# Context attention on one core: score maxima issued eight tiles ahead over each block border, and the second shift turn taken into the preceding block

## The chip, the cores and the metric

The kernel is one program on one core of a Trainium2 chip. The metric is the device time of one execution in microseconds (us). TensorE (PE) does the matmuls and loads their weights (PEld), VectorE (DVE) the reductions, ScalarE (ACT) exponentials and copies. GpSimd and the DMA queues play no part in the stage that is changed.

## The reference, cut to what matters

The program is a two-layer decoder on 1024 tokens of 128 features. The changed stage is the first layer's context attention: 16 heads of 8 features look at 6404 context rows, and all heads share one key and one value projection.

```python
c = jnp.concatenate([mem, kv], axis=1)           # both are the same context
qh = (q @ w_q).reshape(B, L, N_HEAD, D_HEAD).transpose(0, 2, 1, 3)
kvp = c @ w_kv
k, v = (kvp[..., :D_HEAD], kvp[..., D_HEAD:])
attn_score = jnp.einsum('bhid,bjd->bhij', qh, k) / np.sqrt(D_HEAD)
attn_prob = jax.nn.softmax(attn_score, axis=-1)
out = jnp.einsum('bhij,bjd->bhid', attn_prob, v)
```

The two halves of the concatenation are equal, so softmax over one of them gives the same output. The kernel computes exp(score - row maximum) and divides by the sum at the end, so every row's maximum must be known before its exponentials start.

## The kernel before

All of the change lies in `context_attention` (L712). The work is cut into 16 blocks (`NB`), each 8 heads of 128 tokens, so 1024 query columns. Even blocks have their queries and keys on partitions 0 to 63, odd blocks on 64 to 127 (`rows`, L810).

A block needs two passes over the context. The **maximum pass** has 104 tiles (`TILES`), 8 heads by 13 ranges of up to 512 context rows, the last range of a head being 260 wide. `max_tile` (L830) is one matmul on 64 partitions into one of four PSUM places (`PLACES`), and `maximum` (L1065) on VectorE reduces it. After tile 51 and after tile 103, `negate` (L1072) turns the maxima of four heads into a negative shift, in halves A and B. `turn_shift` (L838) transposes such a half with four PE instructions into a place of its own, and `take_shift` (L856) copies it on ScalarE into two rows of the query stack, so that the later score matmul subtracts the maximum by itself.

The **score pass** has 102 steps (`EXPS`): 51 chunks of 128 context rows by 2 halves of the query columns. `score` (L967) is one matmul on 64 partitions into one of three PSUM banks, the exponential of it follows on ScalarE (`exponentiate`, L1045), and `weigh` (L956) multiplies a chunk's probabilities with the values, four column strips at a time. Waits of this pass: score e waits for exponential e - 3 (its bank); scores 0 and 1 of a block wait for shifts A and B; a chunk's first exponential waits for `weigh` of three chunks earlier (the probabilities have three buffers); `weigh` of a chunk waits for both its exponentials. The program order on PE is written out in `attend` (L1015): after step e come the items that `items_at` holds for it, then two `weigh` after each step e with e mod 6 = 2, and one after each with e mod 6 = 5. After step 101 the `weigh` of the last but one chunk follows too, and the very last one comes after step 0 of the next block. After exponential 0 ScalarE takes the finished sums of the block before (`take_acc`, L1041).

Both passes run side by side: while block b is scored, the maxima of block b + 1 are computed. These blocks have different parity, so their matmuls use different halves of the partitions. The 103 tiles 1 to 103 are spread over steps 0 to 99; turn A stands after step 57; tile 0 of block b + 2 comes after step 101, and turn B of block b + 1 after the last `weigh` of block b. Its copy by ScalarE follows exponential 101. The maxima of block 0 come before all scores, from `q_first`, mixed with matmuls and copies for layer 1 (`first_job`, `copy_job`); four of these jobs are held back for the time around turn B of block 0. A place is given in the order of issue (`order`, `place`): the item issued four later waits until it was used (`free_place`, L818), a tile by its reduction, a turned shift by its copy. VectorE takes tiles and negations in strict order. Block 15 has no tiles beside it; there each token tile is finished instead (`finish_tile`).

Of the kernel before, what the change touches and what calls it, by code (L numbers as in the profile page):

```python
# [31 lines left out]
NCH = -(-CTX // P)  # L32
# [679 lines left out]
def context_attention(k):  # L712
# [18 lines left out]
    with ctx:  # L731
# [3 lines left out]
        with ExitStack() as tmp:  # L735
# [11 lines left out]
            shift_ready = {"A": k.sem("shift_a_ready"), "B": k.sem("shift_b_ready")}  # L747
# [25 lines left out]
            NJOBS = KEYS + len(val_jobs)  # L773
            EARLY_JOBS = NJOBS
            HELD = 4
            late_jobs = list(range(EARLY_JOBS, NJOBS))

            TURN_AT, LAST_AT, FIRST_TURN = 28, NCH - 1, 66  # L780
            first = [(0, u) for u in range(FIRST_TURN + 1)] + [(0, "A")] + [(0, u) for u in range(FIRST_TURN + 1, TILES)]


            def border(b):
                return [(b + 1, 0)] if b + 1 < NB else [], [(b, "B")]

            items_at = []
            job_at = {}
            for b in range(NB):
                todo = list(range(1, TILES)) if b + 1 < NB else []  # L790
                count = len(todo)
                for c in range(NCH):
                    now = ([], [])
                    if todo and c < LAST_AT:
                        for j in range(2):
                            n = (count * (2 * c + j + 1)) // (2 * LAST_AT) - (count * (2 * c + j)) // (2 * LAST_AT)
                            now[j].extend((b + 1, u) for u in todo[:n])
                            del todo[:n]
                        if c == TURN_AT:
                            now[1].append((b + 1, "A"))  # L800
                    if late_jobs and c in (12, 38):
                        job_at[b * NCH + c] = late_jobs[0]
                        now[1].append(("job", late_jobs.pop(0)))
                    if c == NCH - 1 and b + 1 < NB:
                        now[1].extend(border(b + 1)[0] + border(b + 1)[1])
                    items_at.append(now)
            order = first + border(0)[0] + border(0)[1] + [x for now in items_at for half in now for x in half]
            place = {x: i for i, x in enumerate(order)}

            def rows(blk):  # L810
# [4 lines left out]
            def bank(item):  # L815
                return max_ps[:, place[item] % PLACES, :]

            def free_place(pe, item):  # L818

                if place[item] < PLACES:  # L820
                    return
                blk, what = order[place[item] - PLACES]
                if blk == "job":
                    pe.wait_ge(job_copied, what + 1)
                elif what in shift_ready:
                    pe.wait_ge(shift_ready[what], blk + 1)
                else:
                    pe.wait_ge(tile_used, blk * TILES + what + 1)
# [17 lines left out]

            def issue(pe, item):
                free_place(pe, item)
                if item[0] == "job":
                    layer1_job(pe, item[1], bank(item))  # L850
                elif item[1] in shift_ready:
                    turn_shift(pe, *item)
                else:
                    max_tile(pe, *item)
# [55 lines left out]
            def layer1_job(pe, i, to):  # L910

                if i < KEYS:
                    c0, cols = key_jobs[i]
                    ins = nc.tensor.matmul(to[:, 0:cols], k.wk1[:], k.ctx_T[:, c0:c0 + cols], start=True, stop=True)
                else:
                    c, m = val_jobs[i - KEYS]
                    n = P if c < NCH - 1 else TAIL
                    for j in range(m):
                        ins = nc.tensor.matmul(to[0:n, j * D:(j + 1) * D], k.ctx_T[:, (c + j) * P:(c + j) * P + n],
                                               k.wv1[:], start=True, stop=True)  # L920
                ins.then_inc(job_ready, 1)
# [93 lines left out]
            def attend(pe, blk):  # L1015

                for e in range(EXPS):
                    score(pe, blk, e)
                    items = items_at[blk * NCH + e // JOBS][e % JOBS]
                    for item in items:  # L1020
                        if item[1] != "B":
                            issue(pe, item)
                    of = e // 6 * 3
                    if e == 0 and blk > 0:
                        weigh(pe, blk - 1, NCH - 1)
                    elif e % 6 == 2 and of > 0:
                        weigh(pe, blk, of - 2)
                        weigh(pe, blk, of - 1)
                    elif e % 6 == 5:
                        weigh(pe, blk, of)  # L1030
                    if blk == NB - 1 and e in TURNED_AT:
                        turn_heads(pe, TURNED_AT[e])
                    if blk == NB - 1 and e in BACK_AT:
                        turn_back(pe, BACK_AT[e])
                    if blk == NB - 1 and e in PROJECTED_AT:
                        project(pe, PROJECTED_AT[e])
                weigh(pe, blk, NCH - 2)
                if blk + 1 < NB:
                    issue(pe, (blk + 1, "B"))

            def take_acc(act, blk):  # L1041
                act.wait_ge(pv_done, (blk + 1) * NCH)
# [2 lines left out]
            def exponentiate(act, blk):  # L1045
                for c in range(NCH):
                    n = P if c < NCH - 1 else TAIL
                    if not (blk == 0 and c < 3):
                        act.wait_ge(pv_done, blk * NCH + c - 2)
                    for j in range(JOBS):  # L1050
                        e = c * JOBS + j
                        act.wait_ge(score_ready, blk * EXPS + e + 1)
                        nc.scalar.activation(probs[0:n, c % 3, j * HALF:(j + 1) * HALF], score_ps[0:n, e % 3, :],  # L1053
                                             ACT.Exp).then_inc(exp_done, 1)
                        if e == 0 and blk > 0:
                            take_acc(act, blk - 1)
                    if c == TURN_AT and blk + 1 < NB:
                        take_shift(act, nc.scalar.copy, blk + 1, "A")
                    if blk * NCH + c in job_at:
                        i = job_at[blk * NCH + c]  # L1060
                        copy_job(act, i, bank(("job", i)))
                if blk + 1 < NB:
                    take_shift(act, nc.scalar.copy, blk + 1, "B")

            def maximum(dve, blk, u):  # L1065

# [18 lines left out]
            with nc.Block() as block:  # L1085
                @block.tensor
                def _(pe):
# [19 lines left out]
                            issue(pe, (0, "A"))  # L1107
                    for i in held_jobs[0:2]:
                        first_job(pe, i)
                    for item in border(0)[0] + border(0)[1]:  # L1110
                        issue(pe, item)
                    for i in held_jobs[2:4]:
                        first_job(pe, i)
# [1288 lines left out]
```

## Time and profile before

| what | value |
|---|---|
| median of three runs | 2043.5 us (2041.26 to 2043.7) |
| span of the profiled execution, first to last instruction | 2039.6 us |
| its busy shares: PE, VectorE, ScalarE | 96%, 77%, 66% |
| mean granted TensorE clock | 0.986 |
| first exponential of block 0, of block 15 | 256.8 us, 1215.4 us |
| copies of shift B, block 0 to block 15 | 255.1 us to 1214.8 us: 15 blocks of 63.98 us |

The profiled execution's own device time is not listed; the timed runs are 1.7 to 4.1 us above its span, which is what lies around the first and the last instruction. A busy share is an average over stages, and PE's ends are modelled because its matmuls are pipelined: starts say more than ends. In a timeline row the figures are the start, the length (of the whole merged stretch, with its count), and in brackets how long the engine had been idle and what ended that. "Idle <-X" names who was waited for. Block and step numbers are not in the rows; they follow from counting the instructions of a line.

### The profile page before, as it was taken

What the parts mean: (1) busy time and instruction counts of PE and PEld (TensorE: products, weight loads), DVE (VectorE), ACT (ScalarE), POOL (GpSimd) and SP (SyncE); (2) the same over time, 40 slices, a digit from 0 to 9 for tenths busy, and PEclk for the clock granted to TensorE, in tenths of its full rate; (3) what the DMA queues carried; (4) which work ended last, traced back from release to release, by engine and by line L of the source; (5) the groups of instructions that cost most, each with busy time, mean ns of one, the idle gap of its engine ahead of it and who ended that gap; (6) DMA issues with size and microseconds to landing.
All of it is one profiled execution on the core that took longest, in us unless ns stands there. A gap on an engine that the chain in (4) does not pass through costs nothing. (4 is left out here: it accounts for less than half of the span.)

```text
span 2039.6 us, 36001 instructions
## 1 busy us (share of the span) xinstructions
PE 1959.2 (96%) x14245; PEld 969.3 (48%) x14245; DVE 1573.2 (77%) x2868; ACT 1355.8 (66%) x2394; POOL 100.9 (5%) x85
## 2 busy tenths in 40 slices
PE   7779999999999999999999999999999998999997
PEld 2225744444444444444444444444344444777755
DVE  7997899999999999999999981233688865444344
ACT  5333488888888888888888887432578874443321
POOL 1661000000000000000000000000200000000000
PEclk8999999999999999999999999999999999999999
DMA  4210000000000000000000000232000000000000
GB/s 148 73 62 0 1 2 2 2 1 2 1 1 2 2 1 2 2 2 1 1 2 1 2 2 1 60 120 65 0 1 1 2 1 0 1 1 1 16 29 28
DMA packets 25043, 32.66 MB, mean 16 GB/s; under 512 B 5967, under 2 KB 20335, under 8 KB 24622
## 3 DMA queue, kind: packets, MB, share of 16 engines
q1 hardware_dynamic: 23694, 28.30, 4.5%
q8 instruction: 111, 1.82, 0.4%
q10 hardware_dynamic: 1184, 2.10, 0.3%
q14 instruction: 54, 0.44, 0.1%
HBM read 29.61 MB, written 0.65 MB: 15 GB/s over the span
## 5 line engine op out<-in xcount | busy, mean ns | idle before, releaser
L1069 DVE TENSOR_REDUCE sb_max_partial<-ps_max_ps 128x1 f32<-128x512 f32 (+1 forms) x1664 | 977.3, 662 | 43.9 <-PE ps_max_ps L836 43.1
L1053 ACT ACTIVATE sb_probs<-ps_score_ps 128x512 f32<-128x512 f32 (+1 forms) x1632 | 875.1, 597 | 117.6 <-PE ps_score_ps L974 71.7
L974 PE MATMUL ps_score_ps<-sb_q_stack,sb_key_stack 64*128 64x512 f32 x1632 | 586.6, 443 | 3.9 <-ACT sb_probs L1053 3.4
L836 PE MATMUL ps_max_ps<-sb_key_stack,sb_q_stack 64*128 64x512 f32 (+1 forms) x1560 | 555.9, 438 | 0.0
L963 PE MATMUL ps_acc_ps<-sb_probs,sb_val_ones 128*32 128x256 f32 x6528 | 465.0, 387 | 0.0
L974 PEld LDWEIGHTS ps_score_ps<-sb_q_stack,sb_key_stack 64*128 64x128 f32 x1632 | 275.8, 183 | 321.5 <-ACT sb_probs L1053 257.2
L836 PEld LDWEIGHTS ps_max_ps<-sb_key_stack,sb_q_stack 64*128 64x128 f32 x1560 | 265.0, 184 | 9.8 <-DVE sb_max_partial L1069 7.5
L963 PEld LDWEIGHTS ps_acc_ps<-sb_probs,sb_val_ones 128*32 128x32 f32 x6528 | 156.3, 108 | 207.7 <-issue 140.5
L1721 DVE TENSOR_REDUCE sb_s_max_partial<-ps_s_ps 128x1 f32<-128x512 f32 x256 | 158.5, 682 | 24.6 <-PE ps_s_ps L1567 24.5
L1708 ACT ACTIVATE sb_s_probs<-ps_s_ps 128x512 f32<-128x512 f32 x256 | 140.8, 597 | 30.8 <-PE ps_s_ps L1595 22.8
L1942 DVE TENSOR_SCALAR_CACHE_REDUCE sb_x_scores<-ps_x_score_ps 128x1024 f32<-128x1024 f32 (+1 forms) x56 | 62.0, 1110 | 69.2 <-PE ps_x_score_ps L1929 69.2
L1977 ACT COPY sb_x_turned<-ps_x_turn_ps 128x512 f32<-128x512 f32 (+1 forms) x52 | 29.5, 568 | 116.8 <-PE ps_x_turn_ps L1967 116.8
L1987 PE MATMUL ps_x_acc_ps<-sb_x_turned,sb_val 128*128 128x256 f32 (+1 forms) x408 | 105.4, 381 | 0.0
L1567 PE MATMUL ps_s_ps<-sb_s_key_stack,sb_s_q_stack 64*128 64x512 f32 x256 | 103.5, 462 | 1.9 <-DVE sb_s_q_stack L1521 1.5
L1595 PE MATMUL ps_s_ps<-sb_s_q_stack,sb_s_key_stack 64*128 64x512 f32 x256 | 103.4, 464 | 0.3 <-ACT sb_s_q_stack L1699 0.2
L1929 PE MATMUL ps_x_score_ps<-sb_key_T,sb_x_q_T 128*128 128x512 f32 (+1 forms) x208 | 97.7, 579 | 1.8 <-DVE sb_x_scores L1942 1.8
L1300 DVE TENSOR_TENSOR sb_e_hidden<-sb_e_hidden,sb_e_gate_rows 128x1024 f32<-128x1024 f32 x30 | 36.7, 1226 | 75.6 <-ACT sb_e_hidden L1292 60.3
L471 PE MATMUL ps_mamba_ps<-sb_xpad,sb_ident 128*128 128x512 f32 x128 | 65.2, 632 | 23.0 <-POOL sb_xpad L536 23.0
L640 ACT ACTIVATE sb_val<-sb_delta,sb_a_neg 128x1024 f32<-128x1024 f32 x32 | 36.6, 1148 | 74.0 <-DVE sb_key_T L697 69.3
L1292 ACT ACTIVATE sb_e_hidden<-ps_e_hid_ps,sb_e_b 128x1024 f32<-128x1024 f32 x34 | 37.9, 1113 | 71.4 <-PE ps_e_hid_ps L1268 71.4
L1606 PE MATMUL ps_s_ps<-sb_s_probs,sb_s_val_ones 128*32 128x256 f32 x1024 | 81.8, 391 | 0.2 <-ACT sb_s_probs L1708 0.2
L536 POOL TENSOR_TENSOR sb_xpad<-sb_key_T,sb_val 128x1024 f32<-128x1024 f32 x31 | 73.9, 2383 | 58.3 <-DVE sb_key_T L697 57.2
(299 smaller groups left out, 1802.7 us busy)
## 6 DMA issues: line engine op xcount, KB each, us to landing
sb_val<-c_rows SPq DMA_DIRECT2D x16, 512.0 KB, 3.6
sb_e_gate_rows<-e_gate_dram SPq DMA_DIRECT2D x15, 512.0 KB, 3.9
sb_e_w<-L_ffn_rW SPq DMA_DIRECT2D x30, 128.0 KB, 2.1
sb_e_w<-L_ffn_W_T SPq DMA_DIRECT2D x24, 128.0 KB, 2.1
sb_ctx_T<-ctx_T SPq DMA_DIRECT2D x1, 1664.0 KB, 7.6
sb_ctx_T<-ctx_T ACTq DMA_DIRECT2D x1, 1538.0 KB, 8.6
sb_x_T<-x_T SPq DMA_DIRECT2D x1, 512.0 KB, 3.8
sb_x_tok<-x ACTq DMA_DIRECT2D x1, 512.0 KB, 11.0
```

What stands on the lines that cost most here:

```text
L836: nc.tensor.matmul(bank((blk, u))[:, 0:n], queries, keys, start=True, stop=True).then_inc(tile_ready, 1)
L963: ins = nc.tensor.matmul(acc_ps[32 * q:32 * q + 32, 0:QUART], k.val_ones[:, v, :], probs[:, v % 3, q * QUART:(q + 1) * QUART], start=(v == ...
L974: nc.tensor.matmul(score_ps[:, e % 3, :], k.key_stack[rows(blk), c * P:(c + 1) * P], q_stack[rows(blk), blk // 2, j * HALF:(j + 1) * HALF] ...
L1053: nc.scalar.activation(probs[0:n, c % 3, j * HALF:(j + 1) * HALF], score_ps[0:n, e % 3, :], ACT.Exp).then_inc(exp_done, 1)
L1069: nc.vector.tensor_reduce(partial[:, blk % 2, h, r:r + 1], bank((blk, u))[:, 0:RANGES[r][1]], AX.X, ALU.max).then_inc(tile_used, 1)
L1567: nc.tensor.matmul(bank((blk, u)), q_stack[rows(blk), blk // 2, t * P:(t + 1) * P], key_stack[rows(blk), blk // 2, r * HALF:(r + 1) * HALF ...
L1595: nc.tensor.matmul(score_ps[:, n % 3, :], key_stack[rows(blk), blk // 2, c * P:(c + 1) * P], q_stack[rows(blk), blk // 2, j * HALF:(j + 1) ...
L1606: ins = nc.tensor.matmul(acc_ps[32 * q:32 * q + 32, 0:QUART], val[:, v, head(blk), :], probs[:, n % BUFS, q * QUART:(q + 1) * QUART], star ...
L1708: nc.scalar.activation(probs[:, n // 2 % BUFS, (e % 2) * HALF:(e % 2 + 1) * HALF], score_ps[:, n % 3, :], ACT.Exp).then_inc(exp_done, 1)
L1721: nc.vector.tensor_reduce(partial[:, blk % 2, t, r:r + 1], bank((blk, u)), AX.X, ALU.max).then_inc(tile_used, 1)
L1929: ins = nc.tensor.matmul(score_ps[:, at % 2, (i % 2) * HALF:(i % 2) * HALF + n], q_T[:, t * P:(t + 1) * P], k.key1_T[:, i * HALF:i * HALF ...
L1987: ins = nc.tensor.matmul(acc_ps[:, p % 2, 0:2 * P], k.val1[0:keys, c, :], turned[0:keys, G % DEPTH, 2 * j * P:2 * (j + 1) * P], start=(c = ...
```

## The change

- The tiles of the next block but one that are issued within a block grow from 1 to 8 (`LEAD` + `KEEP`): tiles 0 to 3, then turn B of the next block, then tiles 4 to 7.
- Turn B is one item of the list now, no longer issued after the block's last `weigh`. Its copy on ScalarE follows the second exponential of the chunk in which the turn stands (`shift_at`), no longer exponential 101.
- Turn A stands after tile 57 (`TURN_AFTER`). Items of a block are spread evenly, 106 over 102 steps. That puts turn A alone after step 49, tiles 58 and 59 both after step 50, tile 103 after step 93, tiles 0 to 3 of block b + 2 after steps 94 to 97, turn B after step 98, tiles 4 and 5 after steps 99 and 100, 6 and 7 both after step 101.
- Block 14, which has no block but one after it, spreads 98 items over 96 steps (`LAST_SLOTS`): tile 103 and turn B both stand after step 95.
- Before block 0 the list around turn B grows in the same way: tiles 0 to 3 of block 1, turn B of block 0, tiles 4 to 7, between held jobs 2 and 3.
- Code for late jobs goes; there were none (`EARLY_JOBS = NJOBS`).

```diff
-            TURN_AT, LAST_AT, FIRST_TURN = 28, NCH - 1, 66
+            TURN_AFTER, FIRST_TURN = 57, 66
+            LEAD, KEEP, LAST_SLOTS = 4, 4, 96
             def border(b):
-                return [(b + 1, 0)] if b + 1 < NB else [], [(b, "B")]
+                ahead = [(b + 1, u) for u in range(LEAD + KEEP)] if b + 1 < NB else []
+                return ahead[:LEAD] + [(b, "B")] + ahead[LEAD:]
...
+            items_at, shift_at = [], {}
             for b in range(NB):
-                todo = list(range(1, TILES)) if b + 1 < NB else []
...
+                todo = []
+                if b + 1 < NB:
+                    todo = [(b + 1, u) for u in range(LEAD + KEEP, TURN_AFTER + 1)] + [(b + 1, "A")]
+                    todo += [(b + 1, u) for u in range(TURN_AFTER + 1, TILES)] + border(b + 1)
+                slots = EXPS if b + 2 < NB else LAST_SLOTS
+                for e in range(EXPS):
+                    now = todo[len(todo) * e // slots:len(todo) * (e + 1) // slots]
+                    shift_at.update({(b, e // JOBS): what for _, what in now if what in shift_ready})
                     items_at.append(now)
...
                 for e in range(EXPS):
                     score(pe, blk, e)
-                    items = items_at[blk * NCH + e // JOBS][e % JOBS]
-                    for item in items:
-                        if item[1] != "B":
-                            issue(pe, item)
+                    for item in items_at[blk * EXPS + e]:
+                        issue(pe, item)
...
                 weigh(pe, blk, NCH - 2)
-                if blk + 1 < NB:
-                    issue(pe, (blk + 1, "B"))
...
-                    if c == TURN_AT and blk + 1 < NB:
-                        take_shift(act, nc.scalar.copy, blk + 1, "A")
...
-                if blk + 1 < NB:
-                    take_shift(act, nc.scalar.copy, blk + 1, "B")
+                    if (blk, c) in shift_at:
+                        take_shift(act, nc.scalar.copy, blk + 1, shift_at[blk, c])
...
-                    for item in border(0)[0] + border(0)[1]:
+                    for item in border(0):
                         issue(pe, item)
```

## Rows read from the trace of the kernel before

**Rows 1.** Busy time by stretch: length, PE, PEld, DVE, ACT, POOL, clock, DMA; block 8.

```profile
768.01:831.94 63.93, 63.51 (x630) 29.05 (x622) 61.90 (x111) 55.97 (x106) 0.00 (x0) 1.00 0.01 2
```

**Rows 2.** Groups by line and shape, block 2: count, busy, mean ns, idle before.

```profile
L1069 DVE TENSOR_REDUCE sb_max_partial<-ps_max_ps 128x1 f32<-128x512 f32 x97 | 59.4, 683 | 2.4 <-PE ps_max_ps L836 2.4
```

**Rows 3.** Who waited for whom, whole span: us in total, times, longest.

```profile
PEld ps_score_ps L974 <- ACT sb_probs L1053: 257.2, 683, 0.6
...
PEld ps_max_ps L836 <- DVE sb_max_partial L1069: 12.0, 62, 0.4
```

**Rows 4.** Timeline of VectorE (start, length, count, idle before): border into block 3.

```profile
448.27 0.69 DVE L1069 TENSOR_REDUCE sb_max_partial<-ps_max_ps 128x1 f32<-128x512 f32 x1 [0.64 <-PE ps_max_ps L836]
449.28 15.18 DVE L1069 TENSOR_REDUCE sb_max_partial<-ps_max_ps 128x1 f32<-128x512 f32 x26 [0.31 <-PE ps_max_ps L836]
```

**Rows 5.** Timeline of PE and ACT, block 3, from after step 26 to after step 32.

```profile
463.05 1.07 PE L963 MATMUL ps_acc_ps<-sb_probs,sb_val_ones 128*32 128x256 f32 x16
464.05 0.49 PE L974 MATMUL ps_score_ps<-sb_q_stack,sb_key_stack 64*128 64x512 f32 x1
464.06 0.50 PE L836 MATMUL ps_max_ps<-sb_key_stack,sb_q_stack 64*128 64x512 f32 x1
464.39 0.39 PE L974 MATMUL ps_score_ps<-sb_q_stack,sb_key_stack 64*128 64x512 f32 x1
464.62 0.39 PE L974 MATMUL ps_score_ps<-sb_q_stack,sb_key_stack 64*128 64x512 f32 x1
464.95 0.64 PE L963 MATMUL ps_acc_ps<-sb_probs,sb_val_ones 128*32 128x256 f32 x8
465.52 0.50 PE L974 MATMUL ps_score_ps<-sb_q_stack,sb_key_stack 64*128 64x512 f32 x1
466.21 0.18 PEld L974 LDWEIGHTS ps_score_ps<-sb_q_stack,sb_key_stack 64*128 64x128 f32 x1 [0.30 <-ACT sb_probs L1053]
466.65 1.07 PE L963 MATMUL ps_acc_ps<-sb_probs,sb_val_ones 128*32 128x256 f32 x16
467.35 0.60 ACT L1053 ACTIVATE sb_probs<-ps_score_ps 128x512 f32<-128x512 f32 x1 [0.15 <-PE ps_acc_ps L963]
```

**Rows 6.** Timeline at the border from block 3 to block 4, from step 98 on.

```profile
507.69 1.07 PE L963 MATMUL ps_acc_ps<-sb_probs,sb_val_ones 128*32 128x256 f32 x16
...
509.04 0.28 PE L836 MATMUL ps_max_ps<-sb_key_stack,sb_q_stack 64*128 64x260 f32 x1
...
509.26 0.39 PE L974 MATMUL ps_score_ps<-sb_q_stack,sb_key_stack 64*128 64x512 f32 x1
509.26 0.18 PEld L836 LDWEIGHTS ps_max_ps<-sb_key_stack,sb_q_stack 64*128 64x128 f32 x1
509.49 0.39 PE L836 MATMUL ps_max_ps<-sb_key_stack,sb_q_stack 64*128 64x512 f32 x1
...
511.08 0.60 PE L843 MATMUL ps_max_ps<-sb_ident,sb_neg_part 128*2 128x128 f32 x4 [0.20 <-DVE sb_neg_part L1082]
...
511.71 0.57 ACT L861 CAST sb_q_stack<-ps_max_ps 2x512 fp32r<-2x512 f32 x1 [0.95 <-PE ps_max_ps L843]
...
512.31 0.60 ACT L1053 ACTIVATE sb_probs<-ps_score_ps 128x512 f32<-128x512 f32 x1
...
513.13 0.60 ACT L1053 ACTIVATE sb_probs<-ps_score_ps 128x512 f32<-128x512 f32 x1
```

**Rows 7.** Timeline of PE around turn A, after step 57 of block 1.

```profile
355.04 0.60 PE L843 MATMUL ps_max_ps<-sb_ident,sb_neg_part 128*2 128x128 f32 x4
355.56 0.49 PE L974 MATMUL ps_score_ps<-sb_q_stack,sb_key_stack 64*128 64x512 f32 x1
```

**Rows 8.** Timeline around turn B of block 0, ahead of the first score.

```profile
254.47 0.60 PE L843 MATMUL ps_max_ps<-sb_ident,sb_neg_part 128*2 128x128 f32 x4
254.58 0.69 DVE L1069 TENSOR_REDUCE sb_max_partial<-ps_max_ps 128x1 f32<-128x512 f32 x1 [0.86 <-PE ps_max_ps L836]
254.91 0.61 PE L919 MATMUL ps_acc_ps<-sb_wv,sb_ctx_T 128*128 128x128 f32 x4
```

More of the change, by code:

```diff
@@ L775, in context_attention @@
             HELD = 4
-            late_jobs = list(range(EARLY_JOBS, NJOBS))
-            TURN_AT, LAST_AT, FIRST_TURN = 28, NCH - 1, 66
+            TURN_AFTER, FIRST_TURN = 57, 66
+            LEAD, KEEP, LAST_SLOTS = 4, 4, 96
             first = [(0, u) for u in range(FIRST_TURN + 1)] + [(0, "A")] + [(0, u) for u in range(FIRST_TURN + 1, TILES)]
             def border(b):
-                return [(b + 1, 0)] if b + 1 < NB else [], [(b, "B")]
-            items_at = []
-            job_at = {}
+                ahead = [(b + 1, u) for u in range(LEAD + KEEP)] if b + 1 < NB else []
+                return ahead[:LEAD] + [(b, "B")] + ahead[LEAD:]
@@ L789, in context_attention @@
+            items_at, shift_at = [], {}
             for b in range(NB):
-                todo = list(range(1, TILES)) if b + 1 < NB else []
[L791 to L805, printed above, removed]
+                todo = []
[6 more added lines that the diff above has]
+                    shift_at.update({(b, e // JOBS): what for _, what in now if what in shift_ready})
@@ L806, in context_attention @@
                     items_at.append(now)
-            order = first + border(0)[0] + border(0)[1] + [x for now in items_at for half in now for x in half]
+            order = first + border(0) + [x for now in items_at for x in now]
             place = {x: i for i, x in enumerate(order)}
@@ L822, in free_place @@
                 blk, what = order[place[item] - PLACES]
-                if blk == "job":
-                    pe.wait_ge(job_copied, what + 1)
-                elif what in shift_ready:
+                if what in shift_ready:
                     pe.wait_ge(shift_ready[what], blk + 1)
@@ L848, in issue @@
                 free_place(pe, item)
-                if item[0] == "job":
-                    layer1_job(pe, item[1], bank(item))
-                elif item[1] in shift_ready:
+                if item[1] in shift_ready:
                     turn_shift(pe, *item)
@@ L1056, in exponentiate @@
                             take_acc(act, blk - 1)
-                    if c == TURN_AT and blk + 1 < NB:
-                        take_shift(act, nc.scalar.copy, blk + 1, "A")
-                    if blk * NCH + c in job_at:
-                        i = job_at[blk * NCH + c]
-                        copy_job(act, i, bank(("job", i)))
-                if blk + 1 < NB:
-                    take_shift(act, nc.scalar.copy, blk + 1, "B")
+                    if (blk, c) in shift_at:
+                        take_shift(act, nc.scalar.copy, blk + 1, shift_at[blk, c])
             def maximum(dve, blk, u):
```

## The prediction, made before the changed kernel ran

> **What bounds the kernel now.** I read the stretches first. A block lasts 63.9 us, and within one VectorE is busy 61.9 us, ScalarE 56.0 us, PE 63.5 us [rows 1]. So VectorE looks like the bound, with 2.4 us of idle in front of full tiles in a block [rows 2], most of it at the border: 0.64 and 0.31 us, after which 26 tiles run without a gap at 0.58 us each [rows 4]. That idle is what the change can take away. Then I asked who holds PE back. If VectorE set the pace, tiles would wait for their places. They did 62 times in the span, 12.0 us in all, about four times and 0.8 us in a block; score loads waited for exponentials 683 times, 257.2 us [rows 3]. So I followed one period of six steps [rows 5]. From the double weigh at 463.05 to the next at 466.65 it is 3.60 us, and it closes on itself without VectorE: the score at 466.21 waits for an exponential, the weigh follows 0.44 us later, and the exponential at 467.35 waits for that weigh. Seventeen such periods are 61.2 us. The loop between PE and ScalarE is thus the bound, and VectorE's 61.5 us (63.9 less 2.4) lies just under it. VectorE's gaps at the border are in large part the loop's own delay, seen from the side.
>
> Relative to a double weigh at 0, a period on PE reads [rows 5]: score and tile at 1.00, 1.34 and 1.57 (a pair after a pause takes 0.34, later ones 0.23), single weigh at 1.90, scores at 2.47 and 2.81, the third at 3.16 because it waits, double weigh at 3.60, its exponential 0.70 later. A tile costs PE nothing here: it starts 0.01 us after the score beside it, since the two use different partitions.
>
> **The change part by part.**
>
> Tiles 0 to 7 of block b + 2 have block b's parity, so they stand on the partitions of the scores they are issued between. Before, one tile a block did: it started 0.23 us after its score, not 0.01 [rows 6]. Now eight do. The two after step 101 and the ones after 99 and 100 meet other waits (below); those after steps 94 to 97 lie in one period. With score and tile 103 at 1.00: score 1.34, tile 1.57, score 1.80, tile 2.03, weigh 2.36, score 2.93, tile 3.27 (0.34 after the pause), score 3.50, tile 3.73, score 98 at 3.96 in place of 3.16. PE's slack in the period was about 0.1 us, so 0.80 arrives. Bounds: 0 if pipelining hid it all, 8 x 0.23 = 1.84 if nothing were hidden anywhere; I take 0.80, the row-by-row sum.
>
> The Trainium skill ("TensorE: Matmul & The Clock Gate", Part 3, The mechanism) says that a weight load overlaps running matmuls only when its row group differs. By that, each such tile would also pay its load, 0.18 us. Here the trace disagrees: the tile's load started with the score at 509.26 on the same partitions, and the tile 0.23 us later [rows 6]. By the rule the border would cost 4 x 0.18 = 0.7 us more; I leave it out of the sum.
>
> Turn B, four PE instructions, moves in front of the double weigh after step 98. Turn A shows its price: 0.52 us from its start to the next pair [rows 7]. Before the weigh it takes the place of a pair that took 0.44: score 3.96, turn 4.29, weigh 4.82. Against 3.60 that is +1.22, and exponential 98 is as late. The turn's place was tile 0's, so it also waits until VectorE has reduced that tile. Tile 103 is in PE at 1.00, VectorE needs its start-up, the negation and tile 0: before, turn B came 2.04 us after tile 103 with the negation between [rows 6], so tile 0 ends at about 1.00 + 2.04 + 0.6 = 3.6, ahead of 4.29. The bound is 0 to 0.6 (one tile late); I take 0.
>
> From the double weigh to the next block: before, 507.69 to exponential 0 at 512.31, 4.62 us, with 0.95 us of ScalarE idle for turn B, and exponential 1 at 5.44 [rows 6]. After: score 99 at 1.00, tile 1.34, score 1.57, tile 1.80, score 2.03, tile 2.27; exponential 99 at 1.53; ScalarE copies B from 2.02 to 2.60 (0.57, rows 6). Tile 7 has B's place, so PE waits for this copy, and behind it in PE's queue stand two weighs and score 0: tile at 2.65, weighs from 3.09 (0.44), score 0 at 4.09, its exponential at about 4.6. The same as before: ScalarE idles about as long, for another reason. Then the last weigh at 4.53, score 1 at 5.10, exponential 1 at 5.62, that is +0.18. VectorE meanwhile runs dry between tiles 3 and 4 and waits again for tile 8, so it brings no lead into the next block: the 1.0 us at the border [rows 4] isn't gained but moved.
>
> Inside a block the work is the same. Turn A keeps its price but stands ahead of a step that carries two tiles and a double weigh, up to 0.5 worse; the steps with two items fall from four to three, and up to 0.8 us of place waits [rows 3] could go. I take -0.1, with -0.8 and +0.5 as ends.
>
> So a border costs 1.22 + 0.18 - 0.1 = 1.3 us, at 14 borders (out of blocks 0 to 13) 18.2 us.
>
> Before block 0, turn B of block 0 now waits for tile 0's reduction, at 254.58 + 0.69 = 255.27 in place of 254.47 [rows 8]. Tile 6 waits for tile 3's reduction, three tiles of 0.6 later, 257.1; tile 7 follows at 257.35, and the two held jobs, which had started at 254.91, at about 257.6. Their copies and the first score wait for them: +2.7 us. Ends 0.8 (only the turn) and 3.
>
> In block 14 turn B follows tile 103 in the same step 95, so PE and everything behind it wait through reduction and negation: turn at 1.57 + 2.04 = 3.61, single weigh at 4.14 in place of 1.90. The double weigh comes at about 5.6, +2.0; the border after it, without turn and tiles, takes about 3.5 to exponential 0 in place of 4.62. Together +1.0, ends -1 and +2.
>
> The sum is 18.2 + 2.7 + 1.0 = 21.9 us. The span of 2039.6 goes to 2061.5; the median stands 3.9 above the span, and nothing outside the stage changes, so 2043.5 + 21.9 = 2065 us. With the ends of the terms, the border between 0.6 and 1.8, it is 8.4 + 0.8 - 1 = 8 to 25 + 3 + 2 = 30, that is 2052 to 2074. Dropped copies and turns: none; the removed late jobs issued nothing, and no DMA moves.
>
> **The rivals.**
>
> VectorE is the bound after all. It stands at 61.9 of 63.9 us [rows 1], and its tiles run at 0.58 us, which makes six in a period of 3.60 hardly distinguishable from the loop's own [rows 4, 5]. Then eight tiles ahead cover the border, and a block loses the 0.95 us of gaps and the cold restart, about 1.1. It decides wherever a score waits behind a tile that waits for its place. Fifteen borders give -17, less 1 to 3 at the start: 2028 us. Against it stand the four place waits in a block. The Trainium skill ("Perfetto Trace Analysis", Identifying the Most-Contended Engine) takes the engine with the highest occupancy as the one to relieve, judging PE by its weight loads; that rule gives this rival.
>
> The unpaired tiles hide in PE's pauses, and the border is neither better nor worse: only turn B's 0.4 and the start remain, gained back by fewer place waits. For it: PE's pauses are long elsewhere. Against: the period has none where the tiles fall. Sum near 0 to +4: 2045 us.
>
> The change doesn't loosen anything and tightens more: turn B waits for a late VectorE (0.6 a border) and the extra items of steps 25, 50 and 76 delay the loop by 0.24 each [rows 6]. That adds 1.3 a border to my 1.3: 2083 us.
>
> The weight loads of tiles on the scores' partitions are exposed: 0.18 us each [rows 6], four in the critical period, 14 borders, 10 us more than my sum: 2075 us. The row above speaks against it, since that load ran beside the score. The rule of the Trainium skill's page "TensorE: Matmul & The Clock Gate" gives this case.
>
> **How the numbers follow.** My forecast has 0.62, VectorE as the bound 0.18, no effect 0.12, the worse case 0.06, exposed loads 0.02. What can be told from no change is 0.2%, 4 us. Faster gets 0.19 (the first rival and a little of the third), same 0.10, slower 0.71. The range for 8 in 10 reaches down through the case of no effect and up to the edge of the worse case: 2039 to 2079; the likeliest case alone has 2052 to 2074.
>
> **What would show it.** Right: blocks of 65.2 us between shift copies in place of 63.98; score and tile starts 0.23 apart at eight tiles of a block; the double weigh after step 98 about 4.8 us after the one before; ScalarE still idle about a microsecond ahead of exponential 0, now behind a weigh and a score; VectorE dry over a microsecond between tiles 3 and 4; the first exponential 2.7 us later. Wrong: blocks under 63.5 us with VectorE running through the border, or a double weigh after step 98 on time, which would mean that the tiles on the same partitions cost PE nothing.

## The result and the profile after

The changed kernel takes 2103.7 us (median of four executions, 2074.4 to 2116.7), the kernel before on the same chip 2043.6 (2041.3 to 2045.2). It is slower by 60 us, where 21.9 had been forecast. The ratio on record is 1.020, with a 95% interval of 1.015 to 1.026. Ratios here and below leave out executions that were set apart as slow, which keeps 2074.4 and 2094.6 here and 2062.6 and 2078.4 in e7, so that the medians of these two sets give more, 1.029 and 1.022. The executions of the changed kernel differ by up to 42 us, for a reason that the profile shows below, so the time at which one is read has to be named: the profiled one took 2112.8 us, its span is 2111.1 (before: 2039.6), its mean granted TensorE clock 0.958 (before: 0.986).

First the clock row of both pages: the span in 40 slices, the granted clock in tenths of full speed. Before, then after:

```profile
PEclk8999999999999999999999999999999999999999
```

```profile
PEclk8999999999999999999999965799999999999999
```

Before, the whole stage shows 9. After, three slices show 6, 5 and 7. These lie at 1214 to 1372 us, where blocks 14 and 15 end the stage. Stretches of the changed kernel: length, busy time of PE, PEld, VectorE, ScalarE and GpSimd, granted clock, DMA. They are block 8, block 14 and block 15 (first exponential to first exponential, block 15 to its last), and the end of block 14 by itself (counts of instructions in brackets):

```profile
782.95:848.12 65.17, 64.82 (x626) 30.47 (x622) 61.90 (x111) 56.22 (x105) 0.00 (x0) 1.00 0.01 1
1174.16:1242.85 68.69, 66.34 (x617) 29.17 (x613) 57.18 (x102) 56.04 (x105) 0.00 (x0) 0.94 0.00 1
1242.85:1356.61 113.76, 113.76 (x558) 47.82 (x554) 10.41 (x42) 56.67 (x103) 0.00 (x0) 0.54 0.00 1
1233.90:1242.85 8.95, 8.95 (x54) 3.49 (x55) 0.00 (x0) 3.81 (x7) 0.00 (x0) 0.51 0.00 0
```

And block 15 of the kernel before:

```profile
1215.37:1284.20 68.83, 68.61 (x558) 31.81 (x550) 10.44 (x42) 55.54 (x103) 0.00 (x0) 1.00 0.01 1
```

Block 15 has the same 558 matmuls and 103 ScalarE instructions before and after. It takes 68.8 us at a granted clock of 1.00 (2.4 GHz) and 113.8 at 0.54, so nearly all of it at 1.2 GHz, with PE shown as busy all the time. By blocks the 71.5 us of span went here:

| stretch | before | after | difference | forecast |
|---|---|---|---|---|
| tile 0 of block 1 on PE to the first exponential | 2.79 | 6.65 | +3.9 | +2.7 |
| blocks 0 to 13, together | 894.65 | 913.45 | +18.8 | +18.2 |
| block 14 | 63.89 | 68.70 | +4.8 | +1.0 |
| block 15 | 68.83 | 113.76 | +44.9 | 0 |
| all else | | | -0.9 | 0 |

The border was as forecast. Timeline of PE, ScalarE (ACT) and VectorE (DVE) of the changed kernel from the double weigh after step 92 of block 3 to the first exponential of block 4 (start, length of the stretch, idle before):

```profile
512.56 1.07 PE L951 MATMUL ps_acc_ps<-sb_probs,sb_val_ones 128*32 128x256 f32 x16
...
513.90 0.39 PE L962 MATMUL ps_score_ps<-sb_q_stack,sb_key_stack 64*128 64x512 f32 x1
514.13 0.39 PE L826 MATMUL ps_max_ps<-sb_key_stack,sb_q_stack 64*128 64x512 f32 x1
514.36 0.39 PE L962 MATMUL ps_score_ps<-sb_q_stack,sb_key_stack 64*128 64x512 f32 x1
514.59 0.39 PE L826 MATMUL ps_max_ps<-sb_key_stack,sb_q_stack 64*128 64x512 f32 x1
...
516.84 0.60 PE L833 MATMUL ps_max_ps<-sb_ident,sb_neg_part 128*2 128x128 f32 x4
517.36 1.07 PE L951 MATMUL ps_acc_ps<-sb_probs,sb_val_ones 128*32 128x256 f32 x16
518.07 0.60 ACT L1037 ACTIVATE sb_probs<-ps_score_ps 128x512 f32<-128x512 f32 x1 [0.91 <-PE ps_acc_ps L951]
519.12 2.48 DVE L1048 TENSOR_REDUCE sb_max_partial<-ps_max_ps 128x1 f32<-128x512 f32 x4 [1.45 <-PE ps_max_ps L826]
519.51 0.57 ACT L849 CAST sb_q_stack<-ps_max_ps 2x512 fp32r<-2x512 f32 x1
520.57 1.07 PE L951 MATMUL ps_acc_ps<-sb_probs,sb_val_ones 128*32 128x256 f32 x16
522.15 0.69 DVE L1048 TENSOR_REDUCE sb_max_partial<-ps_max_ps 128x1 f32<-128x512 f32 x1 [0.54 <-PE ps_max_ps L826]
522.17 0.60 ACT L1037 ACTIVATE sb_probs<-ps_score_ps 128x512 f32<-128x512 f32 x1 [1.00 <-PE ps_score_ps L962]
```

Read it from the weighs. From 512.56 to 517.36 are 4.80 us, where a period takes 3.60 [rows 5]. In between, score and tile alternate 0.23 us apart, since both use the same partitions, and turn B (L833) stands in front of the second weigh. VectorE, which before ran 26 tiles without a gap from behind the border on [rows 4], is dry for 1.45 us there and for 0.54 us at the next tile. ScalarE idles 1.00 us before exponential 0, as it idled 0.95 before the copy of B [rows 6].

Then the place where the clock goes. PE in the changed kernel at the end of block 14, from tile 103 on:

```profile
1231.14 0.28 PE L826 MATMUL ps_max_ps<-sb_key_stack,sb_q_stack 64*128 64x260 f32 x1
1233.54 0.60 PE L833 MATMUL ps_max_ps<-sb_ident,sb_neg_part 128*2 128x128 f32 x4 [2.03 <-DVE sb_neg_part L1061]
1234.08 1.08 PE L951 MATMUL ps_acc_ps<-sb_probs,sb_val_ones 128*32 128x256 f32 x8
1235.09 1.64 PE L962 MATMUL ps_score_ps<-sb_q_stack,sb_key_stack 64*128 64x512 f32 x3
1236.66 1.93 PE L951 MATMUL ps_acc_ps<-sb_probs,sb_val_ones 128*32 128x256 f32 x16
```

Turn B of block 15 stands directly behind tile 103, so PE waits 2.03 us for VectorE's last tile and its negation. The next rows are already slow: a single weigh takes 1.08 us where it took 0.64, and a double one 1.93 where it took 1.07 [rows 5]. The trace has the clock at 1.2 GHz from 1234.0 on, for 112.6 us, that is until 1346.6, ten microseconds before the end of block 15.

### The profile page after: what moved, and what is told of

It is laid out like the page before. It is cut to its first block and busy times, and to the rows that moved or that the text cites. A ratio compares the mean times of both kernels' runs of the same rounds, so it can differ in the third digit from the quotient of the medians.

```text
span 2111.1 us, 36001 instructions
## 1 busy us (share of the span) xinstructions
PE 2030.3 (96%) x14245; PEld 1007.6 (48%) x14245; DVE 1573.1 (75%) x2868; ACT 1359.3 (64%) x2394; POOL 100.8 (5%) x85
## 5 line engine op out<-in xcount | busy, mean ns | idle before, releaser
L962 PE MATMUL ps_score_ps<-sb_q_stack,sb_key_stack 64*128 64x512 f32 x1632 | 613.8, 457 | 3.4 <-ACT sb_probs L1037 3.0
L951 PE MATMUL ps_acc_ps<-sb_probs,sb_val_ones 128*32 128x256 f32 x6528 | 486.3, 402 | 0.0
L962 PEld LDWEIGHTS ps_score_ps<-sb_q_stack,sb_key_stack 64*128 64x128 f32 x1632 | 287.9, 191 | 330.8 <-ACT sb_probs L1037 270.8
L471 PE MATMUL ps_mamba_ps<-sb_xpad,sb_ident 128*128 128x512 f32 x128 | 65.2, 632 | 22.8 <-POOL sb_xpad L536 22.8
```

Of the source, the lines that this page charges most:

```text
L951: ins = nc.tensor.matmul(acc_ps[32 * q:32 * q + 32, 0:QUART], k.val_ones[:, v, :], probs[:, v % 3, q * QUART:(q + 1) * QUART], start=(v == ...
L962: nc.tensor.matmul(score_ps[:, e % 3, :], k.key_stack[rows(blk), c * P:(c + 1) * P], q_stack[rows(blk), blk // 2, j * HALF:(j + 1) * HALF] ...
```

## The experiments

All times are medians, beside the kernel before on the same chip (2042.0 to 2043.9 us). Unless it says otherwise, an edit is one to the changed kernel. "Thin" stands for steps with a score but no tile beside it, so that the scores run on one half of the partitions with nothing on the other, as in all of block 15. A row of blocks has the columns of the stretches above.

### Is it the clock, and what makes it fall?

**e7, the changed kernel once more**, no edit, in a second set of runs.

> The changed kernel as it is, a second time, beside the next three. If the fall of the clock at the end of block 14 belongs to the program, most executions show block 15 near 110 us and times from 2075 to 2115 again (theory P+Q: the wait of 2.0 us together with six steps without tiles). If it was the chip's mood that day (R), the time is about 2066 and block 15 takes 69 us.

2087.1 us (2062.6 to 2123.3), ratio 1.014 (1.009 to 1.019). Blocks 14 and 15 of the profiled execution, which took 2123.3 us:

```profile
1175.51:1244.61 69.10, 66.75 (x617) 29.26 (x613) 57.20 (x102) 56.04 (x105) 0.00 (x0) 0.93 0.00 1
1244.61:1364.74 120.13, 120.13 (x550) 50.16 (x550) 10.42 (x42) 56.88 (x103) 0.00 (x0) 0.50 0.00 1
```

The fall comes again, 1.2 GHz for 133 us this time, and block 15 is 6 us longer still. The kernel before, beside it on the same chip, took 2040.8 to 2045.8 us in seven executions, so it isn't the chip alone. The wait is the same to the hundredth:

```profile
1234.89 1.01 PE L833 MATMUL ps_max_ps<-sb_ident,sb_neg_part 128*2 128x128 f32 x4 [2.03 <-DVE sb_neg_part L1061]
```

The trace has the clock down from 1234.69 on, 0.20 us before this turn starts. So the clock fell within PE's wait, before anything behind it had run. In the first profile it fell 0.46 us behind the wait's end, when PE had begun nothing but turn B.

The eight executions of the changed kernel line up by their mean granted clock: 2123.3 us at 0.954, 2116.7 at 0.957, 2112.8 at 0.958, 2094.6 and 2095.7 at 0.969, 2078.4 at 0.977, 2074.4 at 0.979, 2062.6 at 0.987. The last one has the clock of the kernel before (0.983 to 0.988) and the time that I had forecast. Going by these means (two of the eight have a trace), one execution in eight shows no fall, and the others differ by how long it lasts.

**e1, tile 103 and turn B of block 15 six steps later**, so that no thin steps remain in block 14:

```diff
-            LEAD, KEEP, LAST_SLOTS = 4, 4, 96
+            LEAD, KEEP, LAST_SLOTS = 4, 4, 102
```

> The changed kernel with one number back: the 98 items of block 14 are spread over all 102 steps, so tile 103 stands after step 100 and turn B of block 15 after step 101. Steps without tiles go, PE's wait for the negation (2.03 us before turn B in the changed kernel) stays, shorter by one step, about 1.5 us. Theory P (that wait lets TensorE's clock fall to 1.2 GHz, and block 15, which has no tiles beside its scores, leaves it there): block 15 still takes over 100 us in most executions, time 2090 to 2115. Theory Q (the six steps without tiles lower the clock): block 15 takes 69 us, time about 2067. Theory R (it is the chip's mood, not the kernel): the kernel before, run beside it, shows it as well.

2066.9 us, ratio 1.012 (1.010 to 1.013): by one number, 20 us less than e7 and 37 less than the first set of the changed kernel. A wait of PE is still there, and blocks 14 and 15 run at full clock:

```profile
1238.23 0.60 PE L833 MATMUL ps_max_ps<-sb_ident,sb_neg_part 128*2 128x128 f32 x4 [1.43 <-DVE sb_neg_part L1061]
```

```profile
1176.55:1240.35 63.80, 62.16 (x618) 28.01 (x614) 57.50 (x102) 55.88 (x106) 0.00 (x0) 1.00 0.00 1
1240.35:1309.25 68.90, 68.68 (x558) 31.84 (x550) 10.45 (x42) 55.62 (x103) 0.00 (x0) 1.00 0.00 1
```

So the loss hangs on the steps at which tile 103 and turn B stand. Wait, thin steps, and place were all changed here, and the next runs part them.

**e2, block 14 ends as before**, turn B of block 15 after the last weigh:

```diff
+                if b + 2 == NB:
+                    todo.remove((NB - 1, "B"))
-                slots = EXPS if b + 2 < NB else LAST_SLOTS
+                slots = EXPS if b + 2 < NB else EXPS - 2
...
+                if blk == NB - 2:
+                    issue(pe, (NB - 1, "B"))
...
```

> The changed kernel, but block 14 ends as in the kernel before: 97 items over 100 steps, turn B of block 15 after the last weigh, its copy after the last exponential. Blocks 0 to 13 and the start stay changed. P and Q both expect the clock to stay up: block 15 at 69 us. Then what is left is the 14 borders at 1.3 us (18.3), the start at 3.9 and about nothing in block 14: 2043.6 + 22 = 2066 us. If R holds, block 15 is long in some executions here too.

2063.1 us, ratio 1.009 (1.008 to 1.011); block 14 takes 62.9 us, block 15 70.3. The other borders and the start are as in the changed kernel here. Near the beginning of block 15 the clock falls as well, at 1240.86, but it is back after 3.4 us. PE's only wait in the five microseconds ahead of that is short:

```profile
1238.58 0.99 PE L964 MATMUL ps_score_ps<-sb_q_stack,sb_key_stack 64*128 64x512 f32 x2 [0.21 <-ACT sb_probs L1041]
```

So thin work without a long wait can lose the clock too, and here it got it back within block 15.

**e5, thin steps without the wait**: tile 103 stays after step 95, turn B goes to step 99, where the negation is done.

```diff
+                    if b + 2 == NB:
+                        now = [x for x in now if x[1] != "B"] + ([(NB - 1, "B")] if e == 99 else [])
```

> The changed kernel, but turn B of block 15 stands after step 99, four steps behind tile 103, so that PE does scores and weighs while VectorE reduces and negates. Steps 96 to 101 keep having no tiles. P: no wait of 2 us on PE, the clock stays up, block 14 near 65 us, block 15 at 69 us, time about 2066. Q: the clock falls as in the changed kernel, block 15 over 100 us, time 2090 to 2115.

2065.4 us, ratio 1.011 (1.009 to 1.013).

```profile
1173.88:1237.04 63.16, 62.82 (x617) 28.02 (x613) 57.19 (x102) 56.05 (x105) 0.00 (x0) 1.00 0.01 1
1237.04:1305.95 68.91, 68.69 (x558) 31.79 (x550) 10.45 (x42) 55.64 (x103) 0.00 (x0) 1.00 0.01 1
```

Thin work alone, six steps of block 14 and all of block 15, leaves the clock at 1.00 in this profile, also over the instructions at which it fell in e2, and none of its executions has room for a long fall (2062.2 to 2066.9 us).

**e3, the wait in the kernel before**: there turn B of block 15 is put directly behind tile 103, after step 99.

```diff
+                    if b + 2 == NB and c == 49:
+                        now[1].append((NB - 1, "B"))
...
```

> The kernel before with one border changed: turn B of block 15 directly behind tile 103 after step 99 of block 14, its copy after exponential 99. PE waits there about 2 us for the negation; only steps 100 and 101 have no tile. All other borders are as before. P: the clock falls at the end of block 14, block 15 over 100 us in place of 68.8, time 2080 to 2090. Q and R: block 14 a microsecond or two longer, block 15 at 69 us, time 2044 to 2046.

2047.95 us (ten executions, 2043.8 to 2048.6), ratio 1.0019 (1.0010 to 1.0029).

```profile
1217.90 0.60 PE L845 MATMUL ps_max_ps<-sb_ident,sb_neg_part 128*2 128x128 f32 x4 [1.77 <-DVE sb_neg_part L1086]
```

```profile
1155.21:1220.68 65.47, 63.50 (x624) 28.97 (x620) 61.16 (x109) 56.13 (x106) 0.00 (x0) 1.00 0.01 2
1220.68:1289.58 68.90, 68.68 (x558) 31.83 (x550) 10.45 (x42) 55.62 (x103) 0.00 (x0) 1.00 0.01 1
```

I had expected the fall here, and it didn't come: the wait of 1.77 us costs its own 1.6 us in block 14, two thin steps and block 15 follow it, and the clock stays. None of the ten executions has room for a long fall. So my first theory, that a wait in front of block 15 is enough, doesn't hold for one of 1.77 us.

**e8, the wait without the thin steps**: one more matmul, with no use, on the other half of the partitions beside each score of steps 96 to 101 of block 14.

```diff
+                    if blk == NB - 2 and e >= LAST_SLOTS:
+                        spare = max_ps[:, (place[(NB - 1, "B")] + 1 + e % 2) % PLACES, :]
+                        nc.tensor.matmul(spare, q_stack[rows(NB - 1), (NB - 1) // 2, 0:P], k.key_stack[rows(NB - 1), 0:HALF],
+                                         start=True, stop=True)
```

> The changed kernel with its 2.0 us wait before turn B of block 15, but with six extra matmuls in steps 96 to 101 of block 14, one beside each score on the other partitions, whose results nobody reads: steps as dense as elsewhere. If the wait alone were enough (P), block 15 stays near 110 us and the time between 2075 and 2115. If the wait and the thin steps are both needed (P+Q), the clock stays up: block 15 at 69 us, time 2066 to 2069.

2069.1 us (2061.2 to 2070.6), ratio 1.013 (1.012 to 1.015). The wait is the same to the hundredth, and in the profiled execution the clock stays:

```profile
1230.44 0.60 PE L833 MATMUL ps_max_ps<-sb_ident,sb_neg_part 128*2 128x128 f32 x4 [2.03 <-DVE sb_neg_part L1065]
```

```profile
1171.08:1235.95 64.87, 62.51 (x623) 27.97 (x619) 57.17 (x102) 56.04 (x106) 0.00 (x0) 1.00 0.01 1
1235.95:1304.90 68.95, 68.73 (x558) 31.81 (x550) 10.44 (x42) 55.63 (x103) 0.00 (x0) 1.00 0.01 1
```

More matmuls made block 14 3.8 us shorter (64.87 against 68.69) and block 15, which has no edit, 44.8 us shorter. The profile is of the fastest execution; the other three took 2068.0 to 2070.6 us at mean clocks of 0.981 to 0.984. That leaves room for a short fall in them, as in e11 below (0.980), but not for one of over a hundred microseconds (0.954 and 0.958). So with dense steps behind the same wait the long loss is gone.

That this trace has no fall at all isn't the dense steps' doing, since e7's clock fell before any of them could have run, and up to there this kernel issues what the changed one issues, which also keeps its clock in some executions. Together with e5 and e7 it says: the wait of 2.03 us brings the clock down, the thin work behind it keeps it there, and the long loss needs both.

**e11, dense work in block 15**: such a matmul beside every score of block 15 from step 2 on, block 14 as changed.

```diff
+                    if blk == NB - 1 and e >= 2:
+                        nc.tensor.matmul(max_ps[:, 2 + e % 2, :], q_stack[rows(NB - 2), (NB - 2) // 2, 0:P],
+                                         k.key_stack[rows(NB - 2), 0:HALF], start=True, stop=True)
```

> The changed kernel with its wait and its thin steps at the end of block 14, but with one extra matmul beside each score of block 15 from step 2 on, on the other partitions, results unread. If block 15 stays slow because its work is thin, the clock comes back within its first steps: half clock for under 15 us in place of 113 to 133, block 15 about 72 us, time 2066 to 2075. If the clock, once fallen, stays down for another reason, block 15 is over 100 us as before.

2068.4 us (2063.3 to 2073.7), ratio 1.011 (1.009 to 1.014).

```profile
1176.58:1245.33 68.75, 66.39 (x617) 29.18 (x613) 57.18 (x102) 56.13 (x106) 0.00 (x0) 0.93 0.00 1
1245.33:1316.03 70.70, 70.70 (x658) 32.73 (x654) 10.46 (x42) 55.81 (x103) 0.00 (x0) 0.97 0.01 2
```

Block 14 is the changed kernel's (68.75 us, clock 0.93), and the clock falls at 1236.32, 0.38 us behind the wait's end:

```profile
1235.94 0.68 PE L833 MATMUL ps_max_ps<-sb_ident,sb_neg_part 128*2 128x128 f32 x4 [2.03 <-DVE sb_neg_part L1064]
```

But it is back after 13.7 us, and block 15 takes 70.7 us with 100 matmuls more. Two of the four executions (2063.3 and 2063.4 us, both at 0.987) show no fall by their mean clock, so with the eight of the changed kernel that makes three without one in twelve. Wait and fall together cost 4.9 us in block 14, of which the wait alone is 1.0 (e8), and some 2 in block 15. The other 43 of the 45 are there because block 15's thin work stayed at 1.2 GHz for most of its length, although PE is shown as busy all the time. Thin work doesn't rule out a return: e2's clock came back after 3.4 us, and the changed kernel's at 1346.6, ten microseconds before block 15 ended.

### What does the border cost, and why?

**e6, tiles ahead, but turn B and its copy as before**:

```diff
-                return ahead[:LEAD] + [(b, "B")] + ahead[LEAD:]
+                return ahead + [(b, "B")]
...
+                if blk + 1 < NB:
+                    issue(pe, (blk + 1, "B"))
...
```

> The changed kernel with all eight tiles ahead, but every turn B after the block's last weigh and its copy after the last exponential, as before the change. This leaves the tiles' cost alone. Theory of the prediction: tiles on the scores' partitions after steps 94 to 98 cost 0.9 to 1.0 us a border, the turn's 0.4 goes: blocks 1 to 13 at 64.8 to 65.0 us; the time about 2061, less if the start gets shorter. Rival (turn B before the double weigh is the cost): blocks at 63.9 us as before the change, time about 2046 to 2048.

2060.0 us, ratio 1.008 (1.007 to 1.010). Block 8:

```profile
783.44:848.25 64.81, 64.59 (x630) 30.51 (x622) 61.90 (x111) 56.00 (x105) 0.00 (x0) 1.00 0.00 1
```

The eight tiles cost 0.9 us a border (64.81 less 63.93), and the moved turn the other 0.4 (65.17 less 64.81).

**e4, the eight tiles on the other half of the partitions**, from e5, so that they pair with their scores; from block 2 on, their queries and keys are read from those partitions, so that their maxima are those of other queries:

```diff
+                    side = rows(blk + 1) if blk >= 2 and u < LEAD + KEEP else rows(blk)
+                    queries, keys = q_stack[side, blk // 2, h * P:(h + 1) * P], k.key_stack[side, c0:c0 + n]
```

> As e5_turn_later (turn B of block 15 after step 99), but the eight tiles ahead of blocks 2 to 15 read the other 64 partitions, so that they run beside the scores; their maxima are those of other queries. This leaves out what the same partitions cost. Theory of the prediction (0.80 us of the border from tiles 0 to 3 on the scores' partitions, 0.42 from turn B): double weigh to double weigh over turn B 4.0 us in place of 4.8, blocks 1 to 13 at 64.3 to 64.4 us in place of 65.2, time about 2053. Rival (the tiles' partitions don't matter, the cost is the place behind turn B's copy): blocks stay at 65.0 to 65.2 us, time about 2065.

2055.5 us, ratio 1.006 (1.004 to 1.007). Block 8, and the two double weighs around the tiles at the border from block 3:

```profile
779.83:844.35 64.52, 63.52 (x626) 29.28 (x622) 61.90 (x111) 56.10 (x106) 0.00 (x0) 1.00 0.01 1
```

```profile
512.78 1.07 PE L954 MATMUL ps_acc_ps<-sb_probs,sb_val_ones 128*32 128x256 f32 x16
...
516.89 1.07 PE L954 MATMUL ps_acc_ps<-sb_probs,sb_val_ones 128*32 128x256 f32 x16
```

From weigh to weigh it is 4.11 us in place of 4.80, and the block is 0.65 us shorter than the changed kernel's: 0.69 us a border is the price of tiles that share the scores' partitions.

**e10, the kernel before with VectorE's load halved**: every reduction reads at most 128 columns of its tile.

```diff
-                nc.vector.tensor_reduce(partial[:, blk % 2, h, r:r + 1], bank((blk, u))[:, 0:RANGES[r][1]],
+                nc.vector.tensor_reduce(partial[:, blk % 2, h, r:r + 1], bank((blk, u))[:, 0:min(128, RANGES[r][1])],
```

> The kernel before, with every reduction on VectorE over 128 of a tile's columns in place of up to 512 (the rest is left out, so the maxima are partial). VectorE's load in a block falls to under half. Theory: the loop between PE and ScalarE sets the pace, so the period of six steps stays at 3.60 us; only the place waits (0.8 us a block) and a little of the border go: blocks at 62.8 to 63.3 us in place of 63.9, time about 2028 to 2032. Rival (VectorE was the bound): the period falls well under 3.5 us and blocks under 61 us, time under 2000.

2026.4 us, ratio 0.991 (0.990 to 0.993). Block 8, and two double weighs in it, a period apart:

```profile
760.89:823.71 62.82, 62.61 (x630) 28.36 (x622) 28.06 (x111) 55.92 (x105) 0.00 (x0) 1.00 0.01 2
```

```profile
768.35 1.07 PE L963 MATMUL ps_acc_ps<-sb_probs,sb_val_ones 128*32 128x256 f32 x16
...
771.93 1.07 PE L963 MATMUL ps_acc_ps<-sb_probs,sb_val_ones 128*32 128x256 f32 x16
```

VectorE works 28.1 us in a block in place of 61.9, and the block gets 1.1 us shorter; the period is 3.58 us. The loop between PE and ScalarE is the bound. So 1.1 us a block is about what any lead of the tiles could have given back; that is argued from this run and not run by itself.

**e9, the start in its old order**, from e5: tile 0, turn B, the held jobs, then tiles 1 to 7.

```diff
+                if b == 0:
+                    return ahead[:1] + [(b, "B")] + ahead[1:]
...
-                    for item in border(0):
+                    for item in border(0)[:2]:
                         issue(pe, item)
...
+                    for item in border(0)[2:]:
+                        issue(pe, item)
```

> As e5_turn_later, with the start in the old order: tile 0 of block 1, turn B of block 0, the two held jobs, and only then tiles 1 to 7. Turn and jobs no longer wait for reductions; what is left of the start is PE waiting for tile 3's reduction ahead of score 0, about 1.2 us. From tile 0 of block 1 to the first exponential about 4.0 us, in place of 6.7 (e5) and 2.79 (before); time 2 to 3 us under e5's 2065. If the held jobs were not what the start waits for, it stays at 6 us or more.

2066.4 us, ratio 1.011 (1.009 to 1.012), so no gain on e5, where 2 to 3 us had been expected. From tile 0 of block 1 to the first exponential it is 4.91 us in place of e5's 6.83, but block 0 gives it back, 68.53 us in place of 65.50:

```profile
261.46:329.99 68.53, 68.01 (x619) 31.66 (x623) 63.52 (x114) 56.26 (x105) 0.00 (x0) 0.95 0.01 1
```

The clock stood at 1.2 GHz for 6.8 us from 263.6 on, within block 0; in e5 it did so from 257.3 on, half of it ahead of block 0, which begins at 260.6 there. So it seems that the time saved went to the same 6.8 us of low clock at a costlier place; no profile has this start at full clock.

## Why the prediction was right and wrong

**What bounds the kernel: right.** e10 shows it from the other side: with VectorE at 28 us of 62.8 a period is still 3.58 us. The Trainium skill ("Perfetto Trace Analysis", Identifying the Most-Contended Engine), which gave the rival at 0.18, would have this engine relieved first for its occupancy of 61.9 in 63.9 us; the runs disagree, 1.1 us a block for half its load.

**The border: right, in size and in place.** Forecast 1.3 us, measured 1.29 in blocks 1 to 13 (16.7 over 13). Block 0 has +2.1, of which 1.1 are left in e7 and e8, where no low clock reaches into it. Double weigh to double weigh was forecast at 4.82 us and is 4.80; blocks at 65.2 us, and they are 65.17; VectorE dry for over a microsecond between tiles 3 and 4, and it is 1.45; ScalarE idle about a microsecond before exponential 0, and it is 1.00. Of the parts, the tiles' 0.80 is 0.9 (e6), of which 0.69 hang on the shared partitions (e4), and turn B's 0.4 is 0.4 (e6). The rival that the tiles hide in PE's pauses fell with e6, the one with exposed weight loads with the 0.23 us between score and tile, and the worse case, 2.6 us a border, with blocks of 65.2 us: the time beyond its 2083 has another cause.

**The start: mechanism right, size short.** Forecast +2.7, measured +3.9. In e7 and e8, where the clock did not fall there, the stretch is 5.65 and 5.66 us, +2.9. PE, ScalarE and the clock in the changed kernel show the rest:

```profile
255.34 0.60 PE L833 MATMUL ps_max_ps<-sb_ident,sb_neg_part 128*2 128x128 f32 x4
255.94 1.92 PE L826 MATMUL ps_max_ps<-sb_key_stack,sb_q_stack 64*128 64x512 f32 x4
257.79 1.22 PE L907 MATMUL ps_acc_ps<-sb_wv,sb_ctx_T 128*128 128x128 f32 x4
259.92 0.76 PE L962 MATMUL ps_score_ps<-sb_q_stack,sb_key_stack 64*128 64x512 f32 x1 [0.39 <-issue]
260.71 3.05 ACT L1037 ACTIVATE sb_probs<-ps_score_ps 128x512 f32<-128x512 f32 x6 [0.90 <-PE ps_score_ps L962]
```

Turn B stands at 255.34 as forecast (255.27), the held jobs at 257.79 (257.6). Then the four matmuls of L907 take 1.22 us where they took 0.61 [rows 8], and the first score 0.76: the clock is at 1.2 GHz from 257.8 on for 6.8 us.

**Block 14: the wait was right, its consequence was the failed step.** The prediction says that PE and everything behind it wait through reduction and negation, and prices this as time only: +1.0. At full clock that holds: in e8, with the same wait of 2.03 us (and six matmuls more), block 14 takes 64.87 us, +1.0. In the changed kernel it takes 68.70, since the nine microseconds behind the wait run at 1.2 GHz.

**Block 15: the missing term.** It had no line in the sum, since nothing in it is edited. It cost 44.9 us, two thirds of the difference. What the prediction left out is that every duration it used was taken from rows at a clock of 1.00 [rows 1], and that the change makes a pause in front of the one stretch of the stage where nothing is paired. The numbers to ask for it were there: the end of block 14 was walked through, with a wait of two microseconds and six steps without tiles behind it. None of the rivals had it, and the range ended at 2079. Without the fall the forecast of 2065 would have stood: e1 gives 2066.9 and e5 2065.4, with only the end of block 14 placed otherwise, and the one execution of the changed kernel whose clock stayed took 2062.6. That e5 comes so close is in part luck: its start costs 4.0 in place of 2.7, and its block 14 is 0.7 us shorter than before in place of 1.0 longer.

**What stays open.** The size of the wait from which the clock falls isn't settled: behind 1.43 us (e1, four executions) and 1.77 us (e3, ten) there was no long fall, with thin work behind both; behind 2.03 us, with the changed kernel's block 14, nine of twelve executions show one by their mean clock, e11's short ones included. And e3 differs from the changed kernel also in what stands ahead of its wait. Nor is it settled why three in twelve show no fall, why the others stay down for different times, and what brought the clock back at 1346.6. The Trainium skill ("TensorE: Matmul & The Clock Gate", Part 1) says that the monitor which sets the clock runs free of the program, so that the same kernel changes its clock at other moments from run to run. The spread of 2062.6 to 2123.3 us agrees, and so do the moments of the fall, from 0.20 us before the end of the same wait (e7) to 0.46 us behind it; no run here sets the two against each other on purpose.

## What to carry to other kernels

Where a change makes PE wait, look at what runs behind the wait, not only at how long it is: a stretch that keeps PE on half of its partitions can hold the full clock when it enters with it, and stay at half of it when it doesn't, which here made a wait worth 1 us cost 50. So a stage's last, thin stretch should be entered without a pause, and a forecast for it needs a row for the case that its clock is down. And before work is moved ahead for a busy engine, ask which loop closes on itself: an engine that is busy 97% of a block was worth 1.1 us in 64.

## What the runs showed of the hardware

- The granted clock fell to 1.2 GHz around the end of a PE wait of 2.03 us: 0.46 us behind it (the changed kernel), 0.38 us behind it (e11) and 0.20 us before it (e7). In e8's profiled execution the same wait left it at 2.4 GHz, and so did waits of 1.43 us (e1) and 1.77 us (e3) in theirs.
- It fell for 3.4 us without a long wait too, among scores on 64 partitions and single weighs, with PE idle for 0.21 us in the five microseconds before (e2).
- Block 15's instructions ran 68.8 to 69.0 us at 2.4 GHz (before, e1, e3, e5, e8), and 113.8 and 120.1 us when they began at 1.2 GHz, with PE shown as busy for the whole of them.
- With a second matmul beside each score of block 15 from step 2 on, the clock was back after 13.7 us (e11) in place of 112.6 and 133.1.
- Two matmuls on the same 64 partitions start 0.23 us apart, and on different ones 0.01 [rows 5]; the weight load of the second started together with the first on the same partitions too, at 509.26 [rows 6].
